# Two tiny operations of the attention loop move from ScalarE to VectorE

## The reference

```
xn = layernorm(x)
x  = x + attention(xn) + experts(xn)
attention: qkv = xn @ qkv_w.T; 16 heads of 64; rope on q and k
           scores = q.k / 8 - p[h] * log1p(a[h] * |i - j|)
           out = softmax(scores) @ v, heads joined, @ out_w.T
experts:   top-1 of 16 experts, 256 slots each, two matmuls with relu,
           result times the gate
```

## Time and profile before

| | |
|---|---|
| median of 3 runs | 1268.28 us (1267.39 to 1271.07) |
| the profiled execution, its own time | 1268.28 us |
| its span, first to last instruction | 1266.5 us |
| busy: PE / DVE / ACT / POOL | 1096.5 / 1016.0 / 1002.6 / 818.2 us |
| mean granted TensorE clock | 0.959 of full speed |

### The profile page before, as it was taken

One profiled execution on the slowest core, in us unless ns is written; L12 is line 12 of the kernel. 1 busy time (PEld: TensorE's weight loads), 2 busy tenths in 40 slices (PEclk: granted clock), 3 DMA queues, 4 the chain that ended last, 5 costly groups with the idle time before them and its releaser, 6 DMA issues.

```text
span 1266.5 us, 35475 instructions
## 1 busy us (share of the span) xinstructions
PE 1096.5 (87%) x14436; PEld 798.3 (63%) x14436; DVE 1016.0 (80%) x2061; ACT 1002.6 (79%) x1987; POOL 818.2 (65%) x481
## 2 busy tenths in 40 slices
PE   5740799999479999999999998999999999999874
PEld 5730688898146666666666765666666666666653
DVE  7873799997468788878878887887998788788872
ACT  2684688885169889889889897888998898899991
POOL 3035100000279888898889788888888888888741
PEclk9985799999899999999999999999999999999997
DMA  8715576762126556656755584676567557555573
GB/s 259 273 48 206 182 240 226 236 228 103 33 43 126 110 101 122 131 90 114 131 122 94 114 143 89 102 130 122 102 102 155 98 98 130 127 97 101 111 122 75
DMA packets 390289, 165.79 MB, mean 131 GB/s; under 512 B 340722, under 2 KB 380671, under 8 KB 390128
## 3 DMA queue, kind: packets, MB, share of 16 engines
q1 hardware_dynamic: 377856, 143.26, 53.2%
q0 software_dynamic: 4352, 12.41, 2.9%
q10 hardware_dynamic: 7920, 7.87, 2.0%
HBM read 58.79 MB, written 21.00 MB: 63 GB/s over the span
## 4 chain that ended last, share of the span: by engine, by line
PE 38%; DMA 12%; POOL 9%; ACT 6%; issue 5%; DVE 3%; SPq 1%; another core or an unknown queue 1%; POOLq 0%; ACTq 0%
PE ps_x L1303 9%; PE ps_s L1347 8%; PE ps_o L1378 7%; PE ps_t L1358 6%; PE ps_x L1322 5%; DMA pt_dma<-prob_parts 5%; DMA ot<-ctx_parts 4%; ACT prob L1114 3%; PE ps_x L1313 3%; POOL rot L989 2%; DMA res<-in_L_attn_x_dram 2%; POOL prob_parts L999 2%; POOL got L1016 1%; POOL ctx_parts L1007 1%; ACT pt_pe L1098 1%
## 5 line engine op out<-in xcount | busy, mean ns | idle before, releaser
L1224 DVE CUSTOM_DVE_ANT_0 prob<-ps_s,strips,score_scale 128x512 f32<-128x512 f32 x512 | 360.3, 746 | 10.1 <-PE ps_s L1347 9.4
L1114 ACT ACTIVATE prob<-prob,neg_max 128x512 f32<-128x512 f32 x512 | 364.1, 714 | 2.1
L999 POOL TENSOR_TENSOR prob_parts<-prob,prob_parts 128x1024 f16<-128x1024 f32 x128 | 273.3, 2135 | 84.5 <-ACT prob_parts L1104 84.3
L1230 DVE SCALAR_TENSOR_TENSOR pt_pe<-ps_t,pt_pe 128x1024 f16<-128x1024 f32 x128 | 156.0, 1219 | 54.3 <-ACT pt_pe L1098 54.3
L1347 PE MATMUL ps_s<-parts 32*128 32x512 f16 x3072 | 194.7, 383 | 0.2
L1303 PE MATMUL ps_x<-xcur,wqkv_hi 128*128 128x512 f16 x512 | 156.7, 388 | 36.8 <-ACT proj L1076 20.6
L989 POOL TENSOR_TENSOR rot<-prods 128x1024 f32<-128x1024 f32 x62 | 146.5, 2363 | 12.2 <-DVE parts L1267 11.7
L1358 PEld LDWEIGHTS ps_t<-ident,prob 128*128 128x128 f32 x1024 | 109.8, 141 | 64.0 <-issue 40.2
L1358 PE MATMUL ps_t<-ident,prob 128*128 128x128 f32 x1024 | 139.8, 279 | 8.2 <-DVE pt_pe L1230 8.2
L993 POOL TENSOR_TENSOR parts<-rot,parts 128x1024 f16<-128x1024 f32 x62 | 132.6, 2139 | 6.3 <-ACT parts L1093 6.3
L1104 ACT CAST prob_parts<-prob 128x1024 f16<-128x1024 f32 x128 | 133.7, 1044 | 2.0
(11 more groups left out here) (190 smaller groups left out, 2600.0 us busy)
## 6 DMA issues: line engine op xcount, KB each, us to landing
raw<-in_L_ffn_w_dram SPq DMA_DIRECT2D x32, 1024.0 KB, 5.1
xa<-in_L_attn_x_dram SPq DMA_DIRECT2D x8, 512.0 KB, 6.5
xt_dram<-xth SPq DMA_DIRECT2D x8, 512.0 KB, 5.1
slots_dram<-zeros SPq DMA_DIRECT2D x4, 1024.0 KB, 8.3
xa<-slots_dram SPq DMA_DIRECT2D x16, 256.0 KB, 5.3
expert_dram<-xa POOLq DMA_DIRECT2D x16, 256.0 KB, 6.8
xcur<-xt_dram SPq DMA_DIRECT2D x8, 512.0 KB, 4.3
res<-in_L_attn_x_dram ACTq DMA_DIRECT2D x8, 512.0 KB, 4.0
```

The source lines that it names most:

```text
L999: nc.gpsimd.tensor_tensor(prob_parts[:, n % 2, 1], prob[:, (2 * n + 1) % 3], prob_parts[:, n % 2, 0], ALU.subtract).then_inc(prob_lo, 1)
L1114: nc.scalar.activation(prob[:, s % 3, q, :], prob[:, s % 3, q, :], ACT.Exp, bias=neg_max[:, 2 * (s % 3) + q:2 * (s % 3) + q + 1], scale=-1 ...
L1224: nc.vector.tensor_tensor_reduce(prob[:, s % 3, q, :], ps_s[u][:], strips[:, HG * j + u, start:start + S], score_scale[:, 0:1], 3.0e38, AL ...
L1230: nc.vector.scalar_tensor_tensor(out=pt_pe[:, n % 2, 1].rearrange("p q k c -> p q (k c)"), in0=ps_t[:], scalar=P_SCALE, in1=pt_pe[:, n % 2 ...
```

## The change

`shift` and `scale_sums` go away on ACT. On DVE a `shift` is added behind the fourth `negate` of each quad, ahead of `read_context` and `pair_low`; the scaling of the sums is added inside `read_context`, ahead of the reciprocal, which waits for it. The semaphore `sums_scaled` disappears. DVE waits for its own `negate` before the shift, and for its own scaling before the reciprocal.

```diff
-            def shift(n):
-                act.wait_ge(negated, 4 * n + 4)
-                i = 2 * ((2 * n + 1) % 3)
-                nc.scalar.activation(neg_max[:, i:i + 2], neg_max[:, i:i + 2], ACT.Copy, bias=LOG_P_SCALE).then_inc(shifted, 1)
-
-            def scale_sums(unit):
-                act.wait_ge(exp_done, 8 * unit + 6)
-                nc.scalar.activation(sums[:, unit % 2, :, 0:2], sums_pe[:, unit % 2], ACT.Copy, scale=P_SCALE).then_inc(sums_scaled, 1)
...
                 exponentials(n, 1)
-                shift(n)
-                if n % 2:
-                    scale_sums(n // 2)
                 exponentials(n, 2)
...
+            def shift(n):
+                dve.wait_ge(negated, 4 * n + 4)
+                i = 2 * ((2 * n + 1) % 3)
+                nc.vector.tensor_scalar(neg_max[:, i:i + 2], neg_max[:, i:i + 2], LOG_P_SCALE, None, ALU.add).then_inc(shifted, 1)
+
             def read_context(unit):
                 dve.wait_ge(pv_done, 4 * unit + 4)
-                dve.wait_ge(sums_scaled, unit + 1)
+                nc.vector.tensor_scalar(sums[:, unit % 2, :, 0:2], sums_pe[:, unit % 2], P_SCALE, None, ALU.mult).then_inc(chain, 1)
+                dve.wait_ge(chain, 2 * unit + 1)
                 nc.vector.reciprocal(rsum[:], sums[:, unit % 2].rearrange("p n u -> p (n u)")).then_inc(chain, 1)
-                dve.wait_ge(chain, unit + 1)
+                dve.wait_ge(chain, 2 * unit + 2)
...
                 negate(n, j, t, 3)
+                shift(n)
                 if n % 2 and n >= 3:
                     read_context(n // 2 - 1)
```

More of the change, by code:

```diff
@@ L883, in attention @@
         val_hi = sem("val_hi")
-        shifted, sums_scaled = sem("max_shifted"), sem("sums_scaled")
+        shifted = sem("max_shifted")
         multiplied, rotated = sem("multiplied"), sem("rotated")
```

## The result

The changed kernel takes 1367.87 us (median of 4 runs, 1359.71 to 1370.12), the kernel before 1269.67 us beside it: a ratio of 1.0758, 95% interval 1.0703 to 1.0813. It is 98 us slower, where 68 were predicted; 1367.87 lies just over the range's end of 1362. The profiled execution took 1375.83 us, its span 1374.1.

A forecast was written before the change was run, and what follows sets the result against it. PE sets the pace, with ACT, POOL and DVE close behind. A, B and C, with place 2 at zero, gave 2.27 us per group, x 30 = 68 us: 1336 us, 5.3% slower; range 1266 to 1362.

The forecast's parts named there:

- What DVE takes on undisturbed: Shift and scaling on DVE, with no disturbance by POOL: 40 us more DVE work, +2 us of kernel time.
- no hold: Rival: POOL never delays DVE's added instructions; 1270 us, chance 0.17.
- w: In the attention, DVE's small operation waits on average for half of a POOL operation, POOL being 84% busy: 0.9 us.
- Place 2: 0.21 + 0.9 < 1.15: 0: Third quad of each group: shift plus hold fit in the 1.15 us `pair_low` waits for ACT; costs nothing.
- A: Place 1, second quad of a group: late `pair_low` delays PE's transposes, after slack; 0.95 us per group.
- B: Place 3 into the next place 0: shift and scaling delay DVE's read, after its idle time; 1.01 us per group.
- C: Place 0, first quad of a group: the shift delays the read before PE's fill, slack 0.80; 0.31 us per group.
- the short holds: Rival: POOL's elementwise work lets DVE in between, 0.24 us held per operation; 1.07 us per group, 1300 us, chance 0.24.
- The scaling comes right behind the shift, so I let it pass in the same gap.: On DVE at places 1 and 3: the scaling meets no POOL hold of its own; nothing added.
- The rival of longer holds: POOL's next operation slips between shift and scaling, which waits another 0.9 us at places 1 and 3; 1390 us, chance 0.08.
- ACT's wait for the shift: ACT's exponential of head 2 waits for a late shift, but ACT has idle time at place 0; nothing added.
- ACT's relief, at most 8 us: Rival: earlier ACT copy at place 2 wins 5 us, earlier context DMAs 3 us; 1260 us, chance 0.08.

The follow-up runs named there:

- the idle pair: Kernel before plus one extra 128x2 tensor_scalar on DVE per quad, on a scratch tile, for which nobody waits: 1348.58 us, ratio 1.0612.

## Why the prediction was right in direction and short in size

- **What bounds the kernel.** Held: with the change made in columns PE keeps its 809 busy us of 860 and the time is that of before. PE's thin meetings with DVE were where the loss came in (8.2 to 110.5 us at `pair_low`).
- **What DVE takes on undisturbed, +2 us in all.** Right: in columns it takes 37 us of DVE (40 predicted for the other form), and the time is 0.18% over before, 2 us, as "no hold" had it.
- **POOL holds the added instruction.** Right, and it is the whole loss: without the held form 0.2% is left. The instructions held in the expert stage were the better witness than the prepare stage's. But they were read one-sidedly: the same POOL instruction that held L65 had let L64 by, 0.2 us earlier, and of the eleven L64 that took 0.17 us five ran wholly beside a POOL instruction:

```profile
151.62 0.17 DVE L64 TENSOR_SCALAR expo_e<-expo_e 128x2 int32<-128x2 int32 x1
```
- **w, "half of one POOL instruction".** This is the term that failed. "Place 2: 0.21 + 0.9 < 1.15: 0" supposes that a hold ends with the POOL instruction that runs. At places 0, 1 and 3 that was nearly so: their holds beyond the 0.17 us were 0.48, 0.64 and 1.02 us, and the 68 us given to them measured 56 (4.42% of 1268.6, with the scaling on ACT; 53 by the medians). At place 2, where POOL has up to five instructions to run without a gap, the hold was 3.31 us beyond the 0.17, far over the slack of 1.15, and brought 40 us (3.14%; 42 by the medians) where nothing was counted. 56 + 40, and the scaling's few, make the 98. The second fault is that one group stood for all: in the group that was followed place 2 took 0.43 us, and the zero was right there; the long holds are in the second and third groups of a batch. Nor does the shift come "at any moment", as half of one instruction supposes, but at nearly the same moment of POOL's order in each batch.
- **The slacks.** Put into the prediction's own sum as an estimate, the mean holds measured in the changed kernel give 0.69 us for A, 1.13 for B and nothing for C, 55 us, near the 56 of the run. For place 2 they give 0.21 + 3.31 - 1.15 = 2.37 us, 71 us, where the run lost 40. So the 1.15 us was not all the slack there: behind the 8.95 us PE stood 4.28. Had the prediction known the holds, it would have come out too high.
- **The sum of the short holds.** 0.53 and 0.59 make 1.12 us and not 1.07, so 34 us and 1302; it changes nothing else.
- **"The scaling comes right behind the shift, so I let it pass in the same gap."** Right: 155 to 156 ns, 407 once. Alone it is held too. The rival of longer holds, in which the scaling waits again, did not happen; its time of 1390 lay nearer to the result than 1336, but for another reason.
- **ACT's wait for the shift, "I add nothing".** Too low, it seems; the run that would show it by itself is missing. ACT stood 149 us at it, and the idle pair, for which ACT doesn't wait, lost 78 us (6.12%) where the shift alone lost 93 (7.34%).
- **ACT's relief, at most 8 us.** Measured at 9 us with both operations gone. Nearly as much lay in the wait for the second head, some 7 us, which I had not looked for.
- **Clock.** Not in the sum: PE's longer gaps came with a mean granted clock of 0.96 for 0.99 and 13.5 us more of busy PE.

The Trainium skill (SBUF — State Buffer, section Who interferes with whom) gives the rule by which these forms sort. A DVE instruction in a two-port mode meets GpSimd, and so does one with two inputs in SBUF when GpSimd reads it, while one SBUF input outside those modes doesn't. The traces agree in the four forms that were held, tensor_scalar of two, three and four elements and tensor_tensor (0.95 to 1.55 us in the mean, where no held one stood ahead). One column and the reciprocals of 128x2 and 128x8 were never held (0.14 to 0.21 us each); that fits the rule if they run outside those modes, which that section says of neither by name. I had cited that page for the tensor_scalar and not applied its line on two inputs; it would have spared me the missed expectation. On the length it says that the pair goes to one engine for the whole instruction; here holds went on through up to six instructions of the other engine, and the measurement decides.

## What to carry to other kernels

Before a small operation goes to DVE, look at what POOL does at that moment, not at POOL's mean: find its longest gapless run of instructions at that place, in every kind of group and not in one, and take the hold as up to that whole run if the operation's form is one that POOL holds. The trace of before has these runs: at place 2 they can be read from it. Write it in a form that isn't held (one column at a time cost 0.15 us each here, against 1.5 us for two together), or put it where POOL stands idle. And ask of each dependent wait whether it waits for more than its own data: here that was worth some 7 us, nearly as much as the relieved engine.

## What the runs showed of the hardware that I had not expected

- A 128x2 instruction of 0.17 us was held for 8.97 us, through five POOL instructions, and in another kernel for 11.36 us, through six; a gap of 0.08 us between two of them ended a hold 33 times of 33.
- At gapless boundaries of POOL a held instruction passed in 218 of 276 cases at the first, and in none of 93 at a later one. At the first it went by the pair of POOL instructions (0 of 28 for one pair, 103 of 104 for another).
- A gather on POOL held it only in its last 0.44 us or so: with 0.52 us or more left the instruction took its 0.16 to 0.18 us.
- A tensor_tensor with both inputs in SBUF was held as the tensor_scalar was (1352 and 1532 ns); 128x3 was held as 128x2 (1420 and 1398 ns); a 128x2 reciprocal was not (161 ns).
- The held side alone pays: POOL's instruction took 2137 ns in the changed kernel, and 2135 before.
